# Relation layer: table rows loaded once for a pair of edge tiles

## The reference, cut to what matters

```
rel_in = concat(x[src], x[dst])                  # per edge, 256 values
for r in range(4):
    mask  = edge_type == r
    rel_t = leaky_relu(rel_in @ W_R[r] + b_R[r])
    e     = leaky_relu(concat(rel_t @ W_Q[r] + b_Q[r], rel_t @ W_K[r] + b_K[r]) @ a_w + a_b)
    attn  = softmax of e over the edges of type r with the same dst
    h    += segment_sum((rel_t @ W_V[r] + b_V[r]) * attn, dst)
h = elu(h)
```

## Time and profile before

| what | value |
|---|---|
| median of three runs | 3080.08 us |
| profiled execution, span | 3100.3 us (the profile gives no other time of that execution) |
| PE, DVE, ACT, POOL busy | 67%, 51%, 38%, 54% of the span |
| TensorE clock granted, mean | 0.675 |
| `rel_layer` | from 107 us to about 930 us of the span |
| bytes moved by DMA | 322.44 MB, 104 GB/s |

### The profile page before, as it was taken

How to read it: one execution, slowest core, us unless ns; L and a number is a source line. 1 busy time by engine, 2 the same in 40 slices (tenths; PEclk the granted TensorE clock), 3 DMA queues, 4 the chain that set the end, 5 groups by cost and what they waited for, 6 DMA issues and landing times. The chain is left out here.

```text
span 3100.3 us, 39481 instructions
## 1 busy us (share of the span) xinstructions
PE 2081.7 (67%) x9935; PEld 1679.2 (54%) x9935; DVE 1578.6 (51%) x4421; ACT 1176.2 (38%) x3344; POOL 1685.1 (54%) x1704
## 2 busy tenths in 40 slices
PE   5436777777765778788782356767777656555367
PEld 2235666666654667667671355556655433333267
DVE  4246767676751242423232434657688654444356
ACT  1245556555332223233231344445454322222244
POOL 3366656565104565565643666666646666666600
PEclk9655565656567889889986555555567665565589
DMA  6644444444103223232322444444432222222264
GB/s 223 233 139 128 129 114 136 117 126 115 41 19 86 71 67 80 65 80 65 81 64 73 126 119 120 115 125 123 124 98 70 75 69 78 71 71 72 65 242 141
DMA packets 244614, 322.44 MB, mean 104 GB/s; under 512 B 105346, under 2 KB 160931, under 8 KB 243045
## 3 DMA queue, kind: packets, MB, share of 16 engines
q0 software_dynamic: 66560, 163.90, 18.6%
q1 hardware_dynamic: 177797, 155.67, 16.6%
HBM read 257.60 MB, written 63.38 MB: 104 GB/s over the span
## 5 line engine op out<-in xcount | busy, mean ns | idle before, releaser
L1422 POOL DMA_INDIRECT e_gathered<-msg_src_table,src_idx x416 | 396.6, 953 | 420.9 <-issue 269.2
L703 POOL DMA_INDIRECT e_gathered<-rel_src_table,rel_idx x416 | 433.5, 1042 | 300.3 <-issue 245.6
L1971 POOL DMA_INDIRECT e_kv<-kv_table,src_idx x416 | 410.1, 986 | 275.3 <-issue 195.1
L1985 POOL DMA_INDIRECT rows_by_src<-e_kv,e_row x416 | 419.3, 1008 | 230.2 <-issue 202.0
L2059 PE MATMUL e_ps_q<-e_window,e_spread 64*128 64x128 f32 x1664 | 350.9, 378 | 151.8 <-ACT e_spread L2198 63.6
L2059 PEld LDWEIGHTS e_ps_q<-e_window,e_spread 64*128 64x128 f32 x1664 | 306.9, 275 | 223.8 <-issue 210.9
L2196 ACT ACTIVATE e_spread<-e_offsets,e_minus_lane 64x512 f32<-64x512 f32 x208 | 149.1, 717 | 563.6 <-remote 340.3
L764 PE MATMUL e_ps_r<-e_window,e_spread 64*128 64x128 f32 x832 | 201.0, 413 | 159.3 <-DMA e_window<-rel_dst_table 109.4
L2095 PE MATMUL e_ps_a<-e_onehot,e_weighted 128*128 128x128 f32 (+1 forms) x832 | 185.3, 396 | 144.7 <-issue 67.2
L764 PEld LDWEIGHTS e_ps_r<-e_window,e_spread 64*128 64x128 f32 x832 | 172.3, 304 | 185.5 <-DMA e_window<-rel_dst_table 117.4
L2095 PEld LDWEIGHTS e_ps_a<-e_onehot,e_weighted 128*128 128x128 f32 x832 | 166.5, 297 | 170.9 <-issue 99.3
(11 more groups left out here) (477 smaller groups left out, 4266.0 us busy)
## 6 DMA issues: line engine op xcount, KB each, us to landing
n_rows<-rows_by_src SPq DMA_DIRECT2D x26, 1032.0 KB
e_offsets<-group_offsets SPq DMA_DIRECT2D x208, 128.0 KB
e_keys<-tile_keys SPq DMA_DIRECT2D x104, 128.0 KB
e_window<-rel_dst_table SPq DMA_DIRECT2D x416, 32.0 KB
e_mixed<-in_edge_attr_dram SPq DMA_DIRECT2D x103, 128.0 KB
rel_src_table<-t_up SPq DMA_DIRECT2D x5, 2560.0 KB
e_gathered<-rel_src_table,rel_idx POOLq DMA_INDIRECT x416
e_gathered<-msg_src_table,src_idx POOLq DMA_INDIRECT x416
```

Source lines behind the costliest of these rows:

```text
L703: pool.indirect_dma_start(gathered[:, q % GS, j, :], None, rel_table, bass.IndirectOffsetOnAxis(ap=rel_idx[:, q * J + j:q * J + j + 1], ax ...
L1422: pool.indirect_dma_start(gathered[:, q % GS, j, :], None, msg_table, bass.IndirectOffsetOnAxis(ap=src_idx[:, q * J + j:q * J + j + 1], ax ...
L1971: pool.indirect_dma_start(kv[:, q % RING, j, :], None, kv_table, bass.IndirectOffsetOnAxis(ap=src_idx[:, q * J + j:q * J + j + 1], axis=0) ...
L1985: pool.indirect_dma_start(in_order, bass.IndirectOffsetOnAxis(ap=row[:, q // 2 % RS, q % 2 * J + j:q % 2 * J + j + 1], axis=0), kv[:, slot ...
```

## The change

Keys count from the first node of a pair of tiles (256 edges), so a key lies under 128, and one load of 128 table rows serves both tiles. A step thus has two window loads of 64 KB in place of four of 32 KB; the key row is broadcast to 128 partitions in place of 64; `spread` has 128 partitions; PE's products have 128 rows. The buffer of the same bytes per partition now has six steps in place of three. The key buffers stay two (KS = 2). `BATCH` is 1 and changes nothing. `lay_out` computes both distances, and the branch is chosen by the larger of the tile's distance and half of the pair's. The table has 128 more nodes of zeros at its end.

```diff
 # lay_out, DVE
-                    dve.wait_ge(keyed, 2)
-                    dve.scalar_tensor_tensor(out=key_s[:, :], in0=dl_s[:, :], scalar=float(R), in1=typ_s[:, :],
+                    dve.tensor_tensor(pairs(pl_s), pairs(dst_s), pairs(dst_s)[:, :, 0:1].to_broadcast([Q, J // 2, 2 * P]),
+                                      ALU.subtract).then_inc(keyed, 1)
+                    dve.wait_ge(keyed, 3)
+                    dve.scalar_tensor_tensor(out=key_s[:, :], in0=pl_s[:, :], scalar=float(R), in1=typ_s[:, :],
                                              op0=ALU.mult, op1=ALU.add).then_inc(keyed, 1)
                     dve.tensor_reduce(top_s[:, :], dl_s[:, :], AX.X, ALU.max).then_inc(keyed, 1)
+                    dve.tensor_reduce(pair_s[:, :], pl_s[:, :], AX.X, ALU.max).then_inc(keyed, 1)
+                    dve.wait_ge(keyed, 6)
+                    dve.scalar_tensor_tensor(out=top_s[:, :], in0=pair_s[:, :], scalar=0.5, in1=top_s[:, :], op0=ALU.mult, op1=ALU.max).then_inc(keyed, 1)
 # rel_tables, SP
-                    sp.dma_start(rel_window[NODES * R:(NODES + P) * R, :].rearrange("(p k) f -> p (k f)", k=R), zeros[:, :]).then_inc(pads_st, 16)
+                    for a in (NODES, NODES + P):
+                        sp.dma_start(rel_window[a * R:(a + P) * R, :].rearrange("(p k) f -> p (k f)", k=R), zeros[:, :]).then_inc(pads_st, 16)
 # rel_layer
-            GS, SLOTS, WS, KS, SS, AHEAD = 6, CH + 8, 3, 2, 2, CH + 8
+            GS, SLOTS, WS, KS, SS, AHEAD = 6, CH + 8, 6, 2, 2, CH + 8
+            BATCH, PAIR = 1, 2 * NEAR_KEYS
-            keys, window = tmp("keys", [NEAR_KEYS, KS, GE]), tmp("window", [NEAR_KEYS, WS, J, D])
-            spread = tmp("spread", [NEAR_KEYS, SS, GE])
+            keys, window = tmp("keys", [PAIR, KS, BATCH, GE]), tmp("window", [PAIR, WS, J // 2, D])
+            spread, pair_lane = tmp("spread", [PAIR, SS, GE]), tmp("minus_pair_lane", [PAIR, P // NEAR])
 # rel_layer, SP, load(q)
-                    hold(sp, parted_keys, nw * (q - KS + 1))
-                    sp.dma_start(keys[:, q % KS, :], key_row[q:q + 1, :].broadcast_to([NEAR_KEYS, GE])).then_inc(keys_in[q % KS], 16)
+                    if q % BATCH == 0:
+                        b = q // BATCH
+                        hold(sp, parted_keys, nw * BATCH * (b - KS + 1))
+                        sp.dma_start(keys[:, b % KS, :, :], key_row[q:q + BATCH, :].rearrange("(a g) e -> a g e", a=1).broadcast_to([PAIR, BATCH, GE])).then_inc(keys_in[b % KS], 16)
                     for w in range(nw):
                         at = nw * q + w
                         hold(sp, expanded, at - WS + 1)
-                        for j in range(J):
-                            sp.dma_start(window[:, at % WS, j, :], rel_window[bass.ds(bases[j] * R + w * NEAR_KEYS, NEAR_KEYS), :]).then_inc(win_in[at % WS], 16)
+                        for k in range(J // 2):
+                            sp.dma_start(window[:, at % WS, k, :], rel_window[bass.ds(bases[2 * k] * R + w * PAIR, PAIR), :]).then_inc(win_in[at % WS], 16)
 # rel_layer, PE, expand(q)
-                            mm = pe.matmul(ps_r[q % 3][:, j, :], spread[:, at % SS, j * P:(j + 1) * P], window[:, at % WS, j, :],
+                            mm = pe.matmul(ps_r[q % 3][:, j, :], spread[:, at % SS, j * P:(j + 1) * P], window[:, at % WS, j // 2, :],
 # rel_layer, ACT, spread_out(q)
+                    act.wait_ge(lanes_told, 1)
-                    act.activation(spread[:, at % SS, :], keys[:, q % KS, :], ACT.Abs, bias=key_lane[0:NEAR_KEYS, w:w + 1]).then_inc(parted_keys, 1)
+                    act.activation(spread[:, at % SS, :], keys[:, q // BATCH % KS, q % BATCH, :], ACT.Abs, bias=pair_lane[:, w:w + 1]).then_inc(parted_keys, 1)
 # rel_layer, DVE, at the stage's start
+                dve.scalar_tensor_tensor(out=pair_lane[:, :], in0=iota[:, 0:P:NEAR], scalar=-float(PAIR // NEAR), in1=lane[:, 0:1].to_broadcast([PAIR, P // NEAR]),
+                                         op0=ALU.mult, op1=ALU.subtract).then_inc(lanes_told, 1)
```

More of the change, by code:

```diff
@@ L83, in build @@
     rel_table = dram("rel_src_table", [NODES * R, 2 * D])
-    rel_window = dram("rel_dst_table", [(NODES + P) * R, D])
+    rel_window = dram("rel_dst_table", [(NODES + 2 * P) * R, D])
     msg_table = dram("msg_src_table", [NG * GN, D])
@@ L132, in lay_out @@
             src_i, dst_i, typ_i = (tmp(n, [Q, GE], I32) for n in ("src_i", "dst_i", "typ_i"))
-            w_s, src_s, dst_s, typ_s, dl_s, key_s, idx_s = (tmp(n, [Q, GE]) for n in
-                                                             ("w_s", "src_s", "dst_s", "typ_s", "dl_s", "key_s", "idx_s"))
+            w_s, src_s, dst_s, typ_s, dl_s, pl_s, key_s, idx_s = (tmp(n, [Q, GE]) for n in
+                                                                   ("w_s", "src_s", "dst_s", "typ_s", "dl_s", "pl_s", "key_s", "idx_s"))
             pen, same = tmp("pen", [Q, GE + 1]), tmp("same", [Q, GE + 1])
@@ L138, in lay_out @@
             base_i = tmp("base_i", [Q, J], I32)
-            top_s, far_s, reach = tmp("top_s", [Q, 1]), tmp("far_s", [Q, 1]), tmp("reach", [1, 2])
+            top_s, pair_s, far_s, reach = tmp("top_s", [Q, 1]), tmp("pair_s", [Q, 1]), tmp("far_s", [Q, 1]), tmp("reach", [1, 2])
             late, spread = tmp("late", [1, 2 * NG - 1]), tmp("spread", [1, 1])
@@ L213, in _ @@
                     sp.dma_start(type_row, typ_s[:, :]).then_inc(stored, 16)
-                    sp.wait_ge(keyed, 3)
+                    sp.wait_ge(keyed, 4)
                     sp.dma_start(key_row, key_s[:, :]).then_inc(stored, 16)
@@ L226, in _ @@
                     tiles = lambda a: a[:, :].rearrange("q (j e) -> q j e", e=P)
+                    pairs = lambda a: a[:, :].rearrange("q (k e) -> q k e", e=2 * P)
                     dve.wait_ge(edges_in, 16 * 12)
@@ L333, in _ @@
                         pe.transpose(ps_row[:, n, :], ends[:, n, :], ident[0:Q, 0:Q])
-                    pe.wait_ge(keyed, 5)
+                    pe.wait_ge(keyed, 8)
                     pe.transpose(ps_top[:, 0, :], top_s[:, :], ident[0:Q, 0:Q])
@@ L500, in _ @@
                                      low[:, g % 2, :, :].rearrange("p k f -> p (k f)")).then_inc(low_st[g % 2], 16)
-                    sp.wait_ge(pads_st, 16 * 9)
+                    sp.wait_ge(pads_st, 16 * 10)
                     for s in range(2):
@@ L667, in rel_layer @@
                 ("repeated", "rows_turned", "leaned", "soft", "exped", "back_turned", "attn_ready"))
-            bounded, inverted = sem("bounded"), sem("inverted")
+            bounded, inverted, lanes_told = sem("bounded"), sem("inverted"), sem("lanes_told")
             node_marked, marked, distant, parted_keys, summed, added, shared, parted, tiles_told = (sem(n) for n in
@@ L758, in expand @@
                         at = nw * q + w
-                        pe.wait_ge(win_in[at % WS], 16 * J * (at // WS + 1))
+                        pe.wait_ge(win_in[at % WS], 16 * (J // 2) * (at // WS + 1))
                         pe.wait_ge(spread_made, at + 1)
@@ L915, in spread_out @@
                     at = nw * q + w
-                    act.wait_ge(keys_in[q % KS], 16 * (q // KS + 1))
+                    act.wait_ge(keys_in[q // BATCH % KS], 16 * (q // BATCH // KS + 1))
+                    act.wait_ge(lanes_told, 1)
                     hold(act, spread_made, at)
                     hold(act, expanded, at - SS + 1)
-                    act.activation(spread[:, at % SS, :], keys[:, q % KS, :], ACT.Abs, bias=key_lane[0:NEAR_KEYS, w:w + 1]).then_inc(parted_keys, 1)
+                    act.activation(spread[:, at % SS, :], keys[:, q // BATCH % KS, q % BATCH, :], ACT.Abs, bias=pair_lane[:, w:w + 1]).then_inc(parted_keys, 1)
                     act.wait_ge(parted_keys, at + 1)
```

## The result

The changed kernel takes 3054.6 us (median of 4 runs, 3049.59 to 3059.67), the kernel before 3081.43 us beside it. The ratio is 0.9917, with a 95% interval from 0.9894 to 0.9939: 26.8 us gained, where 5 us were forecast. The time lies 1.4 us outside the range, on the side of rival 3.

A forecast was written before the change was run, and what follows sets the result against it. The prediction took POOL's own gather pace to bound the relation stage; early steps -5.1, middle -2.0, keys +0.9 and `lay_out` +1.4 summed to -4.8 us, giving 3075 us, range 3056 to 3090.

The forecast's parts named there:

- rival 3: Relation stage: SP was the bound, PE's 72.7 us of window waits are lost time; -21 us, 3059 us; chance 0.22.
- 104 steps save 128 us of SP's time, nearly all of it beside other work.: SP's window issues in `rel_layer`: two of four go away, 1.23 us a step, nearly all hidden.
- a move of the stage's end by over 15 us: Relation stage: the forecast is wrong if PE's waits vanish and the stage's end stays or moves by over 15 us.
- SP's step: SP's issues per relation step: 1.23 us saved, about 2.3 us in place of 3.48.
- The slow stretches: SP's slow patches, four window issues taking 9.39 or 6.58 us instead of 2.45: half the issues should take half.
- Early steps: Steps 4 to 22: POOL's six waits behind PE's late windows shrink; -5.1 us, bounds 0 and 11.7.
- Middle: Steps 45 to 50: late windows of step 45 and POOL's 5.54 us wait at step 50; -2.0 us, bounds 0 and 5.2.
- The products: PE's 832 products with 128 rows in place of 64: 0, at most 8 us of cost.
- Keys doubled: Key row broadcast to 128 partitions: 0.43 us a step, uncovered twice; +0.9 us, bounds 0 and 17.
- rival 2: DMA engines: doubled key load slows key and gather landings, nothing gained; +18 us, 3098 us; chance 0.18.
- Six buffers: Window buffers: depth hardly used, as SP's key loads wait for ACT ahead of the windows; counted as nothing.
- lay_out: DVE ends last in `lay_out`; an extra subtraction, reduction and small operation add 1.4 us on the path, bounds 0 and 1.5.

The follow-up runs named there:

- The zeros: Kernel before, upper 64 partitions of window and spread matrix zeroed once, expansion products over 128 partitions: 0.9963 (2743.59 us) on a 2750 us chip, 0.9988 on a slow one.
- split loads: Changed kernel with each 128-row window load issued as two 64-row loads: 0.9947 on a 2750 us chip, 0.9986 (3104.75 us) on a slow one.
- 34 hold-ups: SP waits for three trifling transfers before every third step's windows: kernel before 1.0246 (2819.39 us); on a slow chip changed kernel 0.9967, with four window issues 1.0219.

## Why the prediction was wrong

**The step that failed: "104 steps save 128 us of SP's time, nearly all of it beside other work."** Enough of it was on the path to be worth some 21 us (12 to 30) of the 26.8. I took POOL for the engine that paces the stage from step 23 on, since its gathers followed its own pace of 6.15 us and no wait for PE stood before them, and I put PE's 72.7 us and ACT's 55.8 us of waits behind it. The zeros show how wrong that was: a quicker TensorE, with POOL's gathers untouched, shortened the stage from 622.7 to 612.1 us on a chip of the 2750 us kind. And split loads brought the long stage back on the slow kind (694.8 us, against 662.0 of the changed kernel on the first chip and 690.1 of the kernel before). Rival 3 had the main mechanism and nearly the time: SP was the bound, 3059 us. That its time fits so well is in part luck, as it had no clock in it and only some 6 us for the steps where over 15 us came. The prediction had named a move of the stage's end by over 15 us as the sign that it was wrong; the end moved by 28.4. What I held against it, that POOL waits for PE in none of steps 23 to 46, rests on a view that names only the last release; most of POOL's idle time stands under "issue", a name for no cause seen, and I read it as POOL's own.

**SP's step.** The saving itself was too small in my sum. The changed kernel on the quiet chip issues a step's keys and windows so:

```profile
114.28 0.33 SPq L727 DMA_DIRECT2D e_keys<-tile_keys  x1
114.81 0.86 SPq L732 DMA_DIRECT2D e_window<-rel_dst_table  x2
```

From the start of the keys to the end of the windows are 1.39 us (114.28 to 115.67), against 3.11 before (181.35 to 184.46): 1.7 us saved where I had 1.2. Issuing 128 rows took less than issuing 64: 0.33 against 0.46 us for the keys, and 0.33 against 0.47 us as the median of the window loads' own records. So the split kernels differ from the changed one not in the number of issues alone, but also in that each window issue is longer again; the runs don't part the two.

**The slow stretches.** I saw them, said that half the issues would take half of the time, and let only the windows of steps 4 to 22 and 45 to 50 count. The total was 107 us of excess in SP, now 51, over the whole stage. What such delays cost depends on the slack: 34 hold-ups cost the kernel before 67 us on a chip of the 2750 us kind, and under 34 hold-ups on a slow chip 74 us lie between four and two window issues a step.

**Early steps.** -5.1 forecast, -8.3 measured at step 22, inside the bounds; PE's waits for windows all but gone (3.6 us before 250 us), as said. On the chip of the 2750 us kind the kernel before is at step 22 after 229.6 us and has nothing to win there.

**Middle.** -2.0 forecast, -4.7 measured from step 22 to 50. PE has no gap before the expansion of step 45 (it stood 6.06 us), but POOL still waits 5.48 us at step 50, where I had let that wait shrink: the steps before it are shorter, the wait is not.

**The products.** "0, at most 8" of cost was of the wrong sign: 380 ns instead of 413 in the profile. I compared two means taken at mixed clocks and left the clock out of the bounds. The gain is some ten us on chips of the 2750 us kind (0.9963), and on the others 4 us that can't be told from nothing (0.9988, 0.9972 to 1.0004).

**Keys doubled.** +0.9 forecast, +3.3 measured by the ratio (0 to 6.6) on a chip of the 2750 us kind; rival 2 (+18) fell, and on the first chip too its sign is absent: DVE's waits for gathers fell from 58.6 to 38.9 us and ACT's for keys from 55.8 to 19.2. By the Trainium skill (DMA: Bandwidth & Descriptors, "Issuing engines are not separate DMA queues") transfers of all engines interleave on the same 16 engines; the run agrees with it in sign, if barely (1.0000 to 1.0024), and the effect is small. From the same page of the Trainium skill (DMA: Bandwidth & Descriptors, "Anatomy of one DMA — SWDGE (gpsimd) path") I had used a formula for how long a transfer takes, by which two transfers instead of four change nearly nothing; it is given there for DMAs issued from GpSimd, and SP issues these. The runs put the price on the engine that issues them: 74 us for two issues a step under hold-ups.

**Six buffers** count for nothing: right, by 0.9972 with three and with six on two chips of the 2750 us kind, and by 0.9975 and 0.9967 under hold-ups. **lay_out:** DVE's extra subtraction is there and takes what I said:

```profile
12.10 0.68 DVE L244 TENSOR_TENSOR pl_s<-dst_s 104x512 f32<-104x512 f32 x1
```

and DVE's work in `lay_out` is 1.4 us longer. But POOL's first gather of the stage starts at 107.20 us, before at 107.53, and POOL's wait just before it fell from 43.7 to 42.5 us. The 1.4 us did not reach the stage's start, so this term was wrong by its whole size.

## What to carry to other kernels

A queue that hardly ever waits for a free buffer (13 times in a hundred steps here, against 77 where the same kernel ran without the slow stretches) is late, not early: look at the waits of the issuing engine itself before placing its work "beside" something. Merging transfers buys slack on the engine that issues them, and slack is worth most where that engine is disturbed; measure on more than one chip before believing a gain of some tenths of a per cent. A product over 64 partitions may be cheaper over 128 with zeros, but only where other engines wait for TensorE.

## What the runs showed of the hardware that I had not expected

- The granted clock of TensorE rose with the partitions that its products contract over, at the same count of products: 0.50 to 0.70 in the stretch 250 to 350 us with zeros in the upper half (360 products against 358 of the kernel before on such a chip), and 0.56 to 0.71 in the later stage. The 0.50 is the level of 1.2 GHz; 0.70 is a mean over time at it and at 2.4 GHz.
- Chips differ by 12 to 13% on one kernel (2748 to 2753 us in three sets of runs, 3081 to 3109 in the others). On the slower ones SP's instructions of 29 or 46 ns take about 700 ns in patches that come back mostly after some 15 to 55 recorded instructions, and POOL has pauses over 1.2 us between gathers: 172 us of them in the message stage in the first profile, 60 us on a chip of the other kind. What causes either is open. The queues named "instruction" moved the same on both kinds of chip (1.52 and 1.34 MB), which neither shows nor excludes the loading of code.
- What I took for POOL's own pauses can be an effect of SP: in the relation stage on a chip of the 2750 us kind, gaps over 1.2 us between gathers come to 59 us in the kernel before and to 138 us in the same kernel with SP held up, though nearly all of them stand under "issue" in the profile. On the slow chips they are 143 us before, 118 us in the changed kernel and 151 us with split loads. So most of them stay where SP is early, and neither these nor the message stage's gaps are explained.
- SP's issue of a window load is recorded at a median of 469 ns for 64 rows (kernel before) and 333 ns for 128 rows (changed kernel), on the same kind of chip.
